# Attention and feed-forward on one core: the second batch's feed-forward as seven products of quarters, with the sums for them made on chip

## The reference

```python
x = x + matmul(fake_quant(layernorm(x)), fake_quant(ctx_4096))
y = layernorm(x)
x = x + (matmul(y, kernel) + bias + lora_gated(y) + lora_shared(y))
```

## Time and profile before

| | us |
|---|---|
| median of 3 runs | 1051.88 (1051.62 to 1055.79) |
| the profiled execution | 1053.82 |
| its span | 1052.3 |
| PE busy | 996.7 (95%) |
| DVE busy | 537.4 (51%) |
| ACT busy | 305.5 (29%) |
| POOL busy | 209.8 (20%) |
| mean granted clock of PE | 0.991 |

### The profile page before, as it was taken

How to read it: one execution, slowest core, us unless ns; L and a number is a source line. 1 busy time by engine, 2 the same in 40 slices (tenths; PEclk the granted TensorE clock), 3 DMA queues, 4 the chain that set the end, 5 groups by cost and what they waited for, 6 DMA issues and landing times.

```text
span 1052.3 us, 12182 instructions
## 1 busy us (share of the span) xinstructions
PE 996.7 (95%) x4736; PEld 470.0 (45%) x4759; DVE 537.4 (51%) x761; ACT 305.5 (29%) x234; POOL 209.8 (20%) x231
## 2 busy tenths in 40 slices
PE   2899999999999999999999999989999999999996
PEld 1364444444544444444444344445544444444442
DVE  7766869878364565454414756787442023014010
ACT  4684423444031142132213521353330021012000
POOL 3011000111014013113311634320204004003110
PEclk9999999999999999999999999999999999999998
DMA  9699862679465245447699743665824025014010
GB/s 364 235 312 390 319 271 46 170 143 214 153 221 201 79 160 189 164 156 199 253 293 292 290 181 129 145 143 125 229 101 160 31 98 162 20 33 156 10 46 24
DMA packets 124392, 181.70 MB, mean 173 GB/s; under 512 B 96064, under 2 KB 96064, under 8 KB 111808
## 3 DMA queue, kind: packets, MB, share of 16 engines
q1 hardware_dynamic: 109600, 118.25, 37.9%
q0 software_dynamic: 13600, 58.73, 15.2%
q10 hardware_dynamic: 1152, 4.19, 1.0%
HBM read 128.72 MB, written 29.36 MB: 150 GB/s over the span
## 4 chain that ended last, share of the span: by engine, by line
PE 67%; DVE 11%; DMA 8%; issue 5%; ACT 5%; SPq 2%; POOL 2%; DVEq 0%; POOLq 0%; ACTq 0%
PE psum L1191 16%; PE psum L1193 16%; PE psum L1192 16%; PE psum L1006 14%; DMA stage<-in_w 2%; PE psum L1214 2%; PE psum L1071 1%; DVE hl L1496 1%; DMA stage<-in_ctx_in 1%; DMA xn<-in_x 1%; SPq L365 1%; DMA lhs<-hl 1%; DMA bias_sb<-in_bias 1%; DVE ring L1450 1%; PE psum L1202 1%
## 5 line engine op out<-in xcount | busy, mean ns | idle before, releaser
L1191 PE MATMUL psum<-ring,lhs 128*128 128x512 f16 x1016 | 386.4, 380 | 9.1 <-issue 6.0
L1192 PE MATMUL psum<-ring,lhs 128*128 128x512 f16 x1016 | 386.3, 380 | 0.0
L1193 PE MATMUL psum<-ring,lhs 128*128 128x512 f16 x1016 | 386.3, 380 | 0.0
L1006 PE MATMUL psum<-ring,lhs 128*128 128x512 bf16 x1002 | 228.7, 384 | 4.5 <-DVE ring L1416 2.0
L1191 PEld LDWEIGHTS psum<-ring,lhs 128*128 128x128 f16 x1016 | 99.6, 98 | 131.0 <-issue 8.4
L1006 PEld LDWEIGHTS psum<-ring,lhs 128*128 128x128 bf16 x1024 | 100.9, 99 | 127.8 <-issue 7.4
L1193 PEld LDWEIGHTS psum<-ring,lhs 128*128 128x128 f16 x1016 | 99.6, 98 | 120.7 <-issue 1.4
L1192 PEld LDWEIGHTS psum<-ring,lhs 128*128 128x128 f16 x1016 | 99.7, 98 | 119.6 <-issue 1.4
L1503 DVE SCALAR_TENSOR_TENSOR x<-psum,sc,x 128x512 f32<-128x512 f32 (+1 forms) x64 | 45.3, 745 | 180.4 <-PE psum L1203 179.5
L638 POOL TENSOR_TENSOR x<-x,bias_sb 128x512 f32<-128x512 f32 (+1 forms) x64 | 89.0, 1416 | 185.7 <-ACT x L915 123.6
L774 ACT ACTIVATE ring<-stage,sc 128x2048 f16<-128x2048 f32 x32 | 63.6, 1999 | 207.7 <-PE psum L1193 159.9
(11 more groups left out here) (167 smaller groups left out, 675.1 us busy)
## 6 DMA issues: line engine op xcount, KB each, us to landing
stage<-in_w SPq DMA_DIRECT2D x38, 1024.0 KB, 6.3
stage<-in_ctx_in SPq DMA_DIRECT2D x30, 1024.0 KB, 7.4
out<-x POOLq DMA_DIRECT2D x64, 256.0 KB, 3.5
x<-in_x POOLq DMA_DIRECT2D x8, 1024.0 KB, 11.9
xn<-in_x POOLq DMA_DIRECT2D x8, 1024.0 KB, 7.0
x<-in_x POOLq DMA_DIRECT2D x4, 2048.0 KB, 15.0
lhs<-in_lora_a POOLq DMA_DIRECT2D x4, 1024.0 KB, 12.7
lhs<-in_lora_b SPq DMA_DIRECT2D x4, 1024.0 KB, 8.9
```

The costliest lines, as they stand in the source:

```text
L1006: last = pe.matmul(psum[:, t, :], lhs_q[:, k, t * P:(t + 1) * P], ring_q[:, g, j % 2, u, :], start=(k == 0), stop=(k == KT - 1 and not by_pe))
L1191: pe.matmul(psum[:, t, :], hi, ring[:, g, 0, u, :], start=(kk == 0), stop=False)
L1192: pe.matmul(psum[:, t, :], hi, ring[:, g, 1, u, :], start=False, stop=False)
L1193: last = pe.matmul(psum[:, t, :], lo, ring[:, g, 0, u, :], start=False, stop=False)
```

## The change

Batch 0 is left as it is. In batch 1, phase 2 is one level of Strassen's scheme. The rows y are cut in four quarters (tokens 0 to 511 or 512 to 1023, input features 0 to 1023 or 1024 to 2047), W likewise, and seven products of a quarter or a sum or difference of two quarters replace the eight of the plain scheme. A product is 4 tiles of 128 tokens by 2 halves of 512 columns, eight banks, each of 8 x 3 matmuls. The list of products, and which operands each takes, is `W_OF`, `W_OP`, `QUAD_OF`.

- The y side: 28 units of 128 x 1024 in high and low parts. Eight come from the lower tiles alone (`lower_tile`, `lower_y`); five come from each of four pairs of tiles (`pair_first`, `pair_last` on DVE, `pair_high` on ACT, three sums on POOL in `pair_sums`). 12 units are transposed at once, 16 are saved to `y_scratch` in HBM and transposed back later (`turn_saved`).
- The W side: for products 0 and 1 a plain quarter; for the other five, two quarters are loaded and summed in `stage`, in eight parts of 1024 elements per partition for each product: by POOL for product 2 (`w_sums`), by DVE for products 3 to 6 (`sum_part`). ACT's and DVE's conversions then handle half as much at a time.
- The result: each bank of products 0 to 4 is added into two quarters of the output (`out_both`), of products 5 and 6 into one; the LoRA part (`delta_bank`) goes with products 2, 3, 5 and 6, into a bank of its own for 2 and 3 (`out_delta`).
- The statistics of batch 1 move behind the evictions of phase 1 (`evict1`), and the differences of the A factors that fit the sums of y are made there (`split_gates`).

The core of the diff:

```diff
+        W_OF = [((1, 1),), ((0, 0),), ((1, 0), (0, 0)), ((0, 1), (1, 1)), ((0, 0), (1, 1)), ((0, 0), (0, 1)), ((1, 0), (1, 1))]
+        W_OP = [None, None, ALU.subtract, ALU.subtract, ALU.add, ALU.add, ALU.add]
+        QUAD_OF = [2, 0, 1, 3, 2, 0, 1]
+        OUT_A = [(0, 0), (1, 1), (0, 0), (1, 1), (0, 0), (1, 1), (0, 0)]
+        OUT_B = [(0, 1), (1, 0), (1, 0), (0, 1), (1, 1)]
...
+            return [(t, n) for n in range(2) for t in range(PT)]
...
+            def load_use(f):
...
+                    sp.wait_ge(converted, CONV0 + f - 1)
+            def load_part(m, n, i):
...
+                    for part, (k, c) in enumerate(W_OF[m]):
+                        sp.dma_start(stage[:, f % 2, 2 * part:2 * part + 2, :],
+                                     w_v[2 * c + n, 2 * k + i // 2][:, i % 2 * 2:i % 2 * 2 + 2, :]).then_inc(stage_in[f % 2], 16)
...
+            def load_a_order(i):
...
+                sp.wait_ge(ax_done, n)
+                sp.dma_start(a_st, a_scratch[GPB + GATE_ORDER[i]]).then_inc(a_in, 16)
...
+                pair_units(3)
+                load_a_order(0)
+                sp.wait_ge(unit_lo, TILES + 5 * PT)
+                for v in range(TILES + 5 * PT - 4, TILES + 5 * PT):
+                    sp.wait_ge(unit_out[v % 4], unit_done(v))
+                turn_saved(0, 3, 0)
+                load_parts(2, 0, range(2, 4))
+                load_delta(2)
+                load_parts(2, 1, range(4))
+                load_a_order(1)
+                load_parts(3, 0, range(2))
+                load_a_order(2)
+                load_a_order(3)
+                load_parts(3, 0, range(2, 4))
+                load_delta(3)
...
+            def pair_sums(p):
...
+                pool.wait_ge(yu_in, p + 1)
+                pool.wait_ge(yl_in, p + 1)
+                pool.tensor_tensor(low1, low1, up1, ALU.subtract).then_inc(pair_in, 1)
+                pool.wait_ge(sum_in, PT + p + 1)
+                pool.tensor_tensor(up0, up0, low0, ALU.subtract).then_inc(pair_in, 1)
+                pool.wait_ge(pair_in, 3 * p + 2)
+                pool.tensor_tensor(low0, low0, up1, ALU.add).then_inc(pair_in, 1)
+            def w_sums(m, n):
...
+                    pool.wait_ge(stage_in[f % 2], in_stage(f))
+                    v = stage[:, f % 2, 0:2, :]
+                    pool.tensor_tensor(v, v, stage[:, f % 2, 2:4, :], W_OP[m]).then_inc(w_sum_pool, 1)
...
+            def pair_high(p):
...
+                act.wait_ge(yu_in, p + 1)
+                unit_high(v, xn[:, HD:D])
+                act.wait_ge(sum_in, PT + p + 1)
+                unit_high(v + 1, y_sum)
+                if p + 1 < PT:
+                    root8(PT + p + 1)
+                row_of(PT + p)
+                act.wait_ge(pair_in, 3 * p + 1)
+                unit_high(v + 2, y_low[:, HD:D])
+                act.wait_ge(pair_in, 3 * p + 2)
+                unit_high(v + 3, xn[:, 0:HD])
+                row_of(p)
+                act.wait_ge(pair_in, 3 * p + 3)
+                unit_high(v + 4, y_low[:, 0:HD])
...
+            def product_bank(m, t, n):
...
+                    if t == 0:
+                        w_in_ring(m, n, h)
+                    for u in range(GU):
+                        kk = h * GU + u
+                        hi = q[:, kk, t * P:(t + 1) * P]
+                        lo = q[:, HK + kk, t * P:(t + 1) * P]
+                        pe.matmul(psum[:, bank, :], hi, ring[:, 2 * n + h, 0, u, :], start=(kk == 0), stop=False)
+                        pe.matmul(psum[:, bank, :], hi, ring[:, 2 * n + h, 1, u, :], start=False, stop=False)
+                        last = pe.matmul(psum[:, bank, :], lo, ring[:, 2 * n + h, 0, u, :], start=False,
+                                         stop=(kk == HK - 1 and m < 5))
+                    if h:
+                        last.then_inc(bank_done, 1)
+                    elif t == PT - 1:
+                        last.then_inc(slot_free, 1)
...
+            def lora_sum(i):
...
+                pe.wait_ge(a_in, 16 * (GPB + i + 1))
+                if i == 3:
+                    pe.wait_ge(p_ready, GPB + 1)
+                else:
+                    pe.wait_ge(out_b, at(1, bank // 2, bank % 2) + 1)
...
+                        then(part)
+                        then(dve.bn_aggr(MV8[:, t, :], stats8[:, t, :, :]))
+                        dve.tensor_scalar(VEPS8[:, t:t + 1], MV8[:, t, 1:2], EPS, None, ALU.add).then_inc(var_ready, 1)
...
+            def unit_low(v, src):
...
+                u = units[v % 4]
+                dve.tensor_tensor(u[:, HD:D], src, u[:, 0:HD], ALU.subtract).then_inc(unit_lo, 1)
...
+            def pair_first(p):
+                t, v = PT + p, TILES + 5 * p
+                dve.wait_ge(inv_ready, t + 1)
+                dve.wait_ge(unit_lo, v)
+                dve.tensor_scalar(xn[:, :], x2[:, t, :], MV8[:, t, 0:1], RSTD8[:, t:t + 1],
+                                  ALU.subtract, ALU.mult).then_inc(yu_in, 1)
+                dve.wait_ge(yu_in, p + 1)
+                dve.tensor_tensor(y_sum, xn[:, 0:HD], xn[:, HD:D], ALU.add).then_inc(sum_in, 1)
+                unit_low(v, xn[:, HD:D])
+                unit_low(v + 1, y_sum)
+            def pair_last(p):
+                v = TILES + 5 * p
+                unit_low(v + 2, y_low[:, HD:D])
+                unit_low(v + 3, xn[:, 0:HD])
+                unit_low(v + 4, y_low[:, 0:HD])
+            def sum_part(m, n, i):
...
+                dve.tensor_tensor(v, v, stage[:, f % 2, 2:4, :], W_OP[m]).then_inc(w_sum, 1)
+            def low_part(m, n, i):
...
+                dve.scalar_tensor_tensor(out=lo, in0=src, scalar=CW_ALL, in1=hi,
+                                         op0=ALU.mult, op1=ALU.subtract).then_inc(converted, 1)
...
+            def units_and_two_products():
...
+                low_part(0, 0, 0)
+                low_part(0, 0, 1)
+                for t in range(PT, TILES):
+                    evict1(1, NBLK - 1, t)
+                    if t == PT:
+                        lower_tile(2)
+                        inverse_root8(3)
+                low_part(0, 1, 0)
+                low_part(0, 1, 1)
+                lower_tile(3)
+                inverse_root8(PT)
+                pair_first(0)
+                inverse_root8(PT + 1)
+                pair_last(0)
+                out_both(0, 0)
+                low_part(1, 0, 0)
+                low_part(1, 0, 1)
+                pair_first(1)
+                inverse_root8(PT + 2)
+                pair_last(1)
+                for i in range(1, 4):
+                    out_both(0, i)
+                low_part(1, 1, 0)
+                low_part(1, 1, 1)
+                pair_first(2)
+                inverse_root8(PT + 3)
+                pair_last(2)
+                out_both(0, 4)
+                pair_first(3)
+                pair_last(3)
+                for i in range(5, 8):
+                    out_both(0, i)
+                out_both(1, 0)
+                out_both(1, 1)
+                half_parts(2, 0, 0)
+            def third_product():
...
+                half_parts(2, 1, 0)
+                half_parts(2, 1, 2)
+                out_both(2, 0)
+                product_sum(0)
+                out_both(2, 1)
+                product_sum(1)
+            def late_product(m):
...
+                half_parts(m, 1, 0)
+                out(0)
+                out(1)
+                half_parts(m, 1, 2)
+                out(2)
+                out(3)
+                if m + 1 < PRODUCTS:
+                    half_parts(m + 1, 0, 0)
+                out(4)
+                if m + 1 < PRODUCTS:
+                    half_parts(m + 1, 0, 2)
+                    if m + 1 in (5, 6):
+                        low_delta(m + 1)
+                out(5)
+                out(6)
+                out(7)
```

595 lines of the change are left out of this document (586 added, 9 removed).

## The result

| us | before | after |
|---|---|---|
| median | 1053.26 (1051.62 to 1055.79, 4 runs) | 1140.73 (1135.46 to 1143.20, 4 runs) |
| profiled execution, span | 1053.82, 1052.3 | 1142.85, 1141.3 |
| mean granted clock of PE | 0.991 | 0.948 |

A forecast was written before the change was run, and what follows sets the result against it. PE's matmul count was taken as the bound. PE's end without waits, 994.7, plus waits of 42, 26 and 11 gave 1073.7; 3 for the clock and 9.1 for the end made 1086 us, range 1056 to 1112.

The forecast's parts named there:

- The pace: PE in batch 1's feed-forward: one 128x512 matmul starts every 0.216 us, one of 128x256 takes about 0.109 us.
- the floor: Span if PE never waits in batch 1's phase 2: PE ends at 994.7, plus 9.1 us behind it, 1003.8 us.
- The direction: Whole kernel: slower, chance 0.80; over 48 us of PE waits make the change a loss.
- Hidden: Batch 1's phase 1: 24 statistics and the A differences cost nothing, as DVE waits for PE; POOL's 32 bias additions have 180 us.
- The bound of 16 us: Batch 1's phase 1: statistics and A differences would cost up to 16 us if uncovered.
- Products 0 and 1: Start of phase 2: DVE's list and pairs of 16 us, DVE and POOL taking turns, make PE wait 42 us.
- Product 2: SP's load order and POOL's sums delay W parts, first `lora_sum` and `a_st`: waits 26 us, product ends at 887.
- The cycle of 10 us for a pair of parts: W stage of products 3 to 6, sums on DVE: 0.8 + 5.4 + 1.2 + 1.2 + 1.3 = 10 us.
- the term of 11 us of waits for products 3 to 6: PE in the late products: waits of 4, 0, 4 and 3 us, with SP's twelve transposes between the cycles.
- much slower: Rival, chance 0.13: W stage binds late products, landing of 8 us makes the cycle 12.5, about + 40: 1126.
- SP's transposes, 10 us for four and 11 by the bound: SP's queue in product 2: four transposes from HBM, two of which held it 5.58 us, take together 10 us.
- The 3 us for the half clock: PE behind some eight long gaps: 1.8 us each, half covered by the next wait, 3 to 7, taken as 3.

The follow-up runs named there:

- the run part by part: Changed kernel with VectorE's order sum, low, sum, low instead of sum, sum, low, low from product 3 on, all work kept: 1123.6 us.

## Why the prediction was right and wrong

- **The pace was right, and with it the terms of the floor.** PE starts one matmul of 128x512 each 0.216 us where it has no wait, and the end behind the last matmul took 9.0 us (9.1 forecast).
- **The direction was right for the reason given**: waits above 48 us make the change a loss. They were 94 us in gaps of over 1 us, for 79 forecast. The span lies 137.5 us above the floor of 1003.8: 15.6 at the start, 94 of waits, 28 of clock.
- **"Hidden" failed.** The statistics and A differences in phase 1 were costed at nothing, because DVE waits for PE there. The start came 15.6 us late: 3.2 us in front of `row_terms`, 12.4 behind it, of which 5 to 8 are the hold beside POOL's additions, 3.3 to 5.5 the statistics. The bound of 16 us stood in the text and nothing of it in the sum. The largest part was not even the work that the bound counts: it was a DVE operation that came to lie beside POOL's row, at a place for which the prediction reads no row.
- **Products 0 and 1: places right, waits too long.** They were 31 us for 42 forecast; the lengths, 121.4 us for 125.8, come out nearer only because the slow clock added 8, which is luck. A pair took 14.7 us three times and 18.9 once (16 forecast). The three waits of product 1 were 5.3, 5.0 and 13.8 us instead of 11, 9.5 and 12.4. The contention of DVE and POOL for SBUF, which the Trainium skill has in GPSIMD Engine Reference, section Specifications, without a figure, is confirmed by rows: 3.4 against 1.2 us. The run without the sums prices them, with all that waits for them, at 11 us of product 1; the prediction had the contention at about 15 of the sum.
- **Product 2: places right, waits too long.** Waits of 6.2, 5.8 and 5.7 us at three of the places named (the rest of W's first half, the first `lora_sum`, the second load of `a_st`), 18 us in all for 26 forecast; the third and fourth load of `a_st` cost under 1 us. The length, 82.6 for 84.5, comes out because the clock took 7, and is luck to that extent.
- **The cycle of 10 us for a pair of parts failed**, and with it the term of 11 us of waits for products 3 to 6, which measured 46, with 13 of clock on top. The order sum, sum, low, low makes the cycle 10.0 to 13.4 us, 11.3 at the median; undoing it brought 10.1 and gave 17 us of the total. The prediction added up the steps of one half of `stage` and left out that DVE's list puts the first half's last step behind the second half's first. The rival *much slower* had the W stage as the bound, as it came out, but from a landing of 8 us; it was 6.2 at the median, and the order in DVE's list did the rest. That rival's 1126 is short too.
- **SP's transposes, 10 us for four and 11 by the bound, failed in products 3 and 4.** All twelve took 56 us instead of 30 to 33. Eight of them cost what the earlier trace rows say, one 7.7 us, and the first of each four 7.0 to 9.5, held until the W loads ahead of it had landed or nearly so, which no row of the prediction prices. Leaving all twelve out gives 24 us.
- **The 3 us for the half clock failed.** Phase 2 took 440.0 us; less 318.0 of matmuls and 94.3 of gaps, 27.7 are left, nearly all of it matmuls 0.42 us apart behind a gap. The forecast charged 1.8 us to each of eight gaps and took most of it for covered. There were twelve gaps of 4.3 us or more, the loss behind each was 1.3 to 3.2 us, 2.3 at the mean, and none was covered. It does not follow the gap's length: 1.4 us behind the gap of 13.7, 2.9 behind that of 19.0, 2.6 behind one of 5.1, none behind those of 2.2 and 1.4. The granted clock was 0.76 over 750 to 800 us and 0.52 over 925 to 945.

## What to carry to other kernels

Before an operation is called hidden, look in the trace at the one place where it will lie, and at what POOL does there at that time. In a double-buffered chain of load, sum and two conversions, write out the list of each engine and see whether the first buffer's last step stands behind the second buffer's first: here that order alone made a cycle of 10.1 us one of 11.3, at the median, and cost 17 us. For DMA transposes, ask what was issued just ahead of them in the same queue. Count the gaps and not only their length when the clock is costed. A scheme that saves 12% of the stage's matmuls must pay for a longer chain that feeds PE: with neither sums nor the second quarters in products 3 to 6, this one still took 1092 us, and with all work kept the best was 1107.7.

## What the runs showed of the hardware

- A fast operation of DVE can be shut out by a whole row of POOL additions: 11.04 instead of 0.69 us (int16 to bf16) and 11.69 instead of 1.22 us (an addition of two bf16 groups), each until the eight additions had ended, while f32 operations with two inputs took turns with POOL one by one. Beside other rows of eight the two took 1.1 and 2.2 us. POOL's rows that shut DVE out took 9.8 to 9.9 us each in every run, those that let it in 11.3 to 12.0; what makes a row the one or the other was not found.
- DMA transposes of one size from HBM held SP's queue in the kernel after for 1.7 to 3.3 us each where no W load issued ahead of them was still on its way, and for 7.0 to 9.5 us where four were (512 KB each): in the kernel after and in the run with the transposes in twos, nine first ones in all, each let go of the queue within 1 us of the last load's landing.
- Twelve gaps of 4.3 to 19.0 us in PE's work cost 1.3 to 3.2 us each in slow matmuls behind them (0.42 us apart instead of 0.216), 28 us in all, whatever the gap's length; those of 2.2 and 1.4 us cost none. Below 4 us no length decides: in the run part by part a gap of 2.0 us cost 1.8 and one of 3.1 none.
